# A two-layer decoder on one core: decay sums taken once in retention, context loads moved ahead, the first keys of head attention and its back projection moved

## What is computed

```
dt = softplus(x @ Wa + dt_bias); alpha = exp(-exp(A_log) * dt)
cum_log = cumsum(log(alpha + 1e-08), axis=1)            # over the 56 tokens, per head
log_l = cum_log[..., :, None] - cum_log[..., None, :]
l_mat = where(causal, exp(log_l), 0)
out = (einsum(q, k) * l_mat) @ v
```

## Time and profile before

| | |
|---|---|
| median of 3 runs | 1634.42 us (1632.02 to 1636.08) |
| profiled execution | 1648.23 us, its span 1646.4 us |
| PE busy in the span | 94% |
| retention, first block | 18 to 43 us |
| retention, slots | 43 to 101 us |
| gate and norm | 101 to 113 us |
| context attention | 113 to 291 us |
| head attention | 668 to 1431 us |

### The profile page before, as it was taken

How to read it: one execution, slowest core, us unless ns; L and a number is a source line. 1 busy time by engine, 2 the same in 40 slices (tenths; PEclk the granted TensorE clock), 3 DMA queues, 4 the chain that set the end, 5 groups by cost and what they waited for, 6 DMA issues and landing times. The chain is left out here.

```text
span 1646.4 us, 45308 instructions
## 1 busy us (share of the span) xinstructions
PE 1544.4 (94%) x16414; PEld 1193.2 (72%) x16414; DVE 1121.6 (68%) x1761; ACT 896.3 (54%) x1419; POOL 701.8 (43%) x755
## 2 busy tenths in 40 slices
PE   8998999989999987889999999999999999889998
PEld 4544666679989655457777777777777777668887
DVE  3643545668787468467777777777777777267777
ACT  5463333432222347346666666666666666467776
POOL 0300000577877456443444433444433444166665
PEclk9998999999999999799999999999999999999999
DMA  2028984131110000376655566655556654212211
GB/s 76 1 58 223 249 243 129 39 118 51 64 41 22 1 2 2 90 166 151 145 127 131 129 142 149 147 125 131 129 140 149 149 125 112 52 39 79 69 63 45
DMA packets 53548, 168.84 MB, mean 103 GB/s; under 512 B 12640, under 2 KB 25280, under 8 KB 53472
## 3 DMA queue, kind: packets, MB, share of 16 engines
q1 hardware_dynamic: 51312, 156.30, 38.0%
q10 hardware_dynamic: 2160, 11.52, 2.3%
HBM read 90.27 MB, written 1.03 MB: 55 GB/s over the span
## 5 line engine op out<-in xcount | busy, mean ns | idle before, releaser
L1907 DVE TENSOR_REDUCE hat_tops<-banks 128x1 f32<-128x500 f32 x672 | 442.0, 677 | 151.4 <-PE banks L1653 151.3
L1780 ACT ACTIVATE hat_pb<-banks 125x896 f32<-125x896 f32 x384 | 340.2, 916 | 226.3 <-PE banks L1672 222.2
L1653 PE MATMUL banks<-hat_kh,hat_qm 128*128 128x500 f32 x672 | 298.7, 462 | 3.8 <-DVE hat_tops L1907 3.5
L1672 PEld LDWEIGHTS banks<-hat_q,hat_k 128*125 128x125 f32 x1536 | 219.6, 188 | 74.4 <-issue 31.9
L1672 PE MATMUL banks<-hat_q,hat_k 128*125 128x224 f32 x1536 | 250.5, 286 | 15.8 <-ACT hat_pb L1780 9.2
L1849 POOL CAST hat_kh<-hat_kf 128x500 fp32r<-128x500 f32 x96 | 58.5, 609 | 404.1 <-ACT hat_kf L1793 389.3
L1663 PE MATMUL banks<-hat_pb,hat_vs 125*27 125x168 f32 (+1 forms) x6144 | 166.9, 261 | 0.1
L1663 PEld LDWEIGHTS banks<-hat_pb,hat_vs 125*27 125x27 f32 (+1 forms) x6144 | 132.1, 98 | 44.1 <-issue 24.4
L1226 ACT ACTIVATE ffn_rg<-banks 128x448 f32<-128x448 f32 x128 | 69.9, 546 | 165.6 <-PE banks L1159 165.5
L1653 PEld LDWEIGHTS banks<-hat_kh,hat_qm 128*128 128x128 f32 x672 | 127.7, 191 | 40.9 <-DVE hat_tops L1907 25.5
L2149 DVE TENSOR_TENSOR moe_hl<-moe_hf,moe_hh 128x448 fp32r<-128x448 f32 x128 | 108.5, 887 | 42.3 <-POOL moe_hh L2041 41.6
(11 more groups left out here) (286 smaller groups left out, 3091.3 us busy)
## 6 DMA issues: line engine op xcount, KB each, us to landing
hat_k<-hat_kh SPq DMA_DIRECT2D x256, 187.5 KB, 4.7
hat_ct<-ctxT SPq DMA_DIRECT2D x32, 750.0 KB, 6.2
hat_k<-hat_kl SPq DMA_DIRECT2D x128, 187.5 KB, 4.5
ctx_cx<-ctx SPq DMA_DIRECT2D x32, 672.0 KB
ctx_cd<-ctxT ACTq DMA_DIRECT2D x15, 750.0 KB, 5.7
ffn_cb<-expert_weights SPq DMA_DIRECT2D x8, 896.0 KB, 4.3
moe_cb<-expert_weights SPq DMA_DIRECT2D x8, 896.0 KB, 6.1
moe_raw<-Mw SPq DMA_DIRECT2D x18, 256.0 KB, 3.0
```

The source lines that it names most:

```text
L1653: peak_out.inc(nc.tensor.matmul(g.bank(PK + m % 2)[:, 0:SB], qm[u][:].rearrange("p h i -> p (h i)")[:, r * 128:r * 128 + 128], kh[u][:, c ...
L1672: mm = nc.tensor.matmul(g.bank(2 * (t % 2) + j // 2)[0:SW, (j % 2) * QW:(j % 2 + 1) * QW], k3[u][:, j, t * SW:(t + 1) * SW], q3[u][:, j, : ...
L1780: exped.inc(nc.scalar.activation(pb[t % 6][:].rearrange("p (n i) -> p n i", n=2), g.ps[0:SW, 2 * (t % 2):2 * (t % 2) + 2, 0:2 * QW], ACT.E ...
L1907: peaked.inc(v.tensor_reduce(tops[:, r, n:n + 1], g.bank(PK + m % 2)[:, 0:SB], AX_X, ALU.max))
```

## The change

It has five parts. (1) The running sums of `decay` are made for all pairs at once: one product by `until`, two copies of the sum (a rounded part and the remainder, `parts`), four transposes, a copy `turned`, a store of it to a DRAM tensor, and from there two small loads for each pair into rows 56 to 59 of `hid[u]`, which also holds the mask. The exponent of a pair is then `unit @ hid` plus `turned @ head_of`, four fp32r products; `after`, `upto`, `dm` and DVE's product are gone. (2) The slots of retention are written out in full. (3) The context loads of pairs 0 to 3 are issued by SP in retention's first block, ahead of the store. (4) In head attention the three key products of sequence 0 follow the first three query products, into banks 4 to 6, and ACT's key copies stand between its query copies; `keep_warm` at the end of causal attention goes. (5) Head attention's output matrix is applied to chunks 0 to 2 before the barrier, in place of the two `keep_warm`s, and the next norm does only chunk 3.

```diff
@@ Normal.on_pe
-            back(0)
-            back(1)
+            for c in range(self.early, max(self.early, 2)):
+                back(c)
         for c in range(CH):
-            if self.project:
-                pe.wait_ge(self.added, c + 1)
+            if self.project and c >= self.early:
+                pe.wait_ge(self.added, c + 1 - self.early)
@@ retention, first block, SP
+                ahead.first_loads(sp)
+                sp.wait_ge(sums_kept, 1)
+                sp.dma_start(g.sums_dram.rearrange("g r c -> r g c"), turned[:].bitcast(F32)).then_inc(sums_stored, 16)
+                sp.wait_ge(sums_stored, 16)
+                sp.wait_ge(cleared, 6)
+                for p in range(2):
+                    load_rows(sp, p)
@@ retention, first block, PE
                     if p == 8:
+                        pe.wait_ge(scaled, 3)
+                        pe.wait_ge(s_step, 6)
+                        nc.tensor.matmul(g.bank(4)[:, 0:PAIRS * H], c_["until"], decay[:]..., start=True, stop=True).then_inc(sums_out, 1)
...
+                pe.wait_ge(sums_split, 2)
+                for n in range(4):
+                    mm = nc.tensor.transpose(g.bank(5)[:, n * 128:n * 128 + 128], parts[:, 4 * n:4 * n + 4]..., c_["ident"])
+                mm.then_inc(sums_turned, 1)
@@ retention, second block, SP
+                for p in range(2, PAIRS):
+                    d_out.wait(sp, p - 2)
+                    load_rows(sp, p)
@@ load_rows
+            for k in range(2):
+                source = g.sums_dram[p // 4, 32 * (p % 4):32 * (p % 4) + 32, 64 * k:64 * k + L]
+                sp.dma_start(hid[p % 2][L + 2 * k:L + 2 * k + 2].bitcast(F32), source.rearrange("(l h) i -> l h i", l=2)).then_inc(rows_in[p % 2], 16)
@@ retention, second block, PE
                         exped.wait(pe, p - 1)
+                        pe.wait_ge(rows_in[u], 32 * (h + 1))
                         for k in range(2):
-                            nc.tensor.matmul(g.ps[:, 4 + k, 0:CW], unit[:], hidden[:], start=True, stop=False)
-                        dmade.wait(pe, p)
+                            nc.tensor.matmul(g.ps[:, 4 + k, 0:CW], unit[:], hid[u][:, 8 * k:8 * k + 8, :], start=True, stop=False)
                         for k in range(2):
-                            mm = nc.tensor.matmul(g.ps[:, 4 + k, 0:CW], c_["after"], dm[u][:, 8 * k:8 * k + 8, :], start=False, stop=True)
+                            mm = nc.tensor.matmul(g.ps[:, 4 + k, 0:CW], turned[own_rows, p // 4, :], head_of[own_rows, 8 * k:8 * k + 8, :], start=False, stop=True)
                         d_out.inc(mm)
@@ context_attention, first block
-            block.sync(first_loads)
@@ causal_attention, end of PE
-                keep_warm(g, 0, 2)
@@ head_attention, PE, query(c)
+                    if c == 0:
+                        pe.wait_ge(loaded[0], 16)
+                    if c < 3:
+                        pe.wait_ge(norm.logged, c + 1)
+                        k_out.inc(nc.tensor.matmul(g.bank(4 + c)[:, 0:SB], g.w["HWkT"][:], ct[0][:, c * SB:(c + 1) * SB], start=True, stop=True))
@@ head_attention, end of PE
-                exped.wait(pe, B - 1)
-                keep_warm(g, 0, 2)
+                normed.wait(pe, B - 9)
+                ends.on_pe(0, 4)
                 sum_weights(B - 1)
-                keep_warm(g, 0, 3)
+                ends.on_pe(1, 5)
+                ends.on_pe(2, 0)
@@ head_attention, end of DVE
                 pick(B - 1)
+                ends.on_dve(dve, 0, 4)
                 divide(B - 1)
+                ends.on_dve(dve, 1, 5)
+                ends.on_dve(dve, 2, 0)
                 normed.wait(dve, B - 1)
+                dve.wait_ge(ends.added, 3)
@@ head_attention, DVE at the start
-                norm.on_dve(dve)
+                norm.on_dve(dve, add_bias)
@@ experts_silu
-        norm = Normal(g, ctx, "n6", ..., g.obias[:, 0:1], split=True)
+        norm = Normal(g, ctx, "n6", ..., g.obias[:, 0:1], split=True, early=3)
```

More of the change, by code:

```diff
@@ L262, in on_dve @@
                 self.parts(dve, 0)
+            if then and c >= 1:
+                then(c - 1)
+        if then:
+            then(CH - 1)
     def parts(self, dve, c):
@@ L356, in _, with retention @@
             dve.wait_ge(normed, CH)
-def retention(g):
+def retention(g, ahead):
     nc, c_ = g.nc, g.c
@@ L582, in _ @@
             def _(dve):
-                give(dve, dmade, weighed)
+                give(dve, weighed)
                 def slot(p, u, h, scores, sums, outputs):
[L586 to L589, removed]
                     if sums:
@@ L661, in context_attention @@
         zt = g.xn
-        cx = [[sb(f"cx{w}{k}", [SW, ST, D]) for k in range(2)] for w in range(4)]
-        cd = [sb(f"cd{u}", [128, 3, SB]) for u in range(2)]
+        cx, cd, loaded, straight = ahead.cx, ahead.cd, ahead.loaded, ahead.straight
         ct = sb("ct", [128, 3, SB])
@@ L727, in slot @@
                         pved.wait(sp, p - 4)
-                        load(sp, p, w)
+                        ahead.load(sp, p, w)
                 four_ends(sp, slot)
@@ L1647, in peak @@
                         qm_made.wait(pe, q)
+                        if isinstance(q, int) and q == 0:
+                            k_full.wait(pe, q)
                     if r == 0:
@@ L1764, in _, with copy_keys @@
                 give(act, v_copied, k_full, exped, logged, inverted)
+                def copy_keys(p, n):
+                    k_out.wait(act, p, n + 1)
+                    k_low.wait(act, p - 1, n + 1)
+                    first = isinstance(p, int) and p == 0
+                    k_full.inc(nc.scalar.activation(kf[:, n * SB:(n + 1) * SB], g.bank(4 + n if first else MISC)[:, 0:SB], ACT.Identity, bias=g.w["Hbk"][:, 0:1]))
                 norm.on_act(act)
                 for c in range(CH):
+                    if c < 3:
+                        copy_keys(0, c)
                     act.wait_ge(q_full, c + 1)
@@ L1788, in copy_values @@
                                                 g.bank(MISC)[0:SW, :].rearrange("p (t h e) -> p t h e", t=4, e=DH)))
[L1790 to L1793, removed]
                 def slot(p, u, h, keys, maxima, sums):
+                    later_keys = keys and reached(p, 1)
                     for i in range(IT):
@@ L1803, in slot @@
                             copy_values(p - 1, 1 - u, 2)
-                        if i == 2 and keys:
+                        if i == 2 and later_keys:
                             copy_keys(p, 1)
@@ L1929, in _, with each_pair @@
                 pick(B - 1)
+                ends.on_dve(dve, 0, 4)
                 divide(B - 1)
+                ends.on_dve(dve, 1, 5)
+                ends.on_dve(dve, 2, 0)
                 normed.wait(dve, B - 1)
+                dve.wait_ge(ends.added, 3)
+def each_pair(engine, slot):
+    for p in range(PAIRS + 2):
+        slot(p, p % 2, p // 2, p < PAIRS, 1 <= p <= PAIRS, p >= 2)
 def staged(engine, n, slot):
```

135 lines of the change are left out of this document (97 added, 38 removed).

## The result

The changed kernel took 1675.97 us (median of 4 runs, 1666.34 to 1678.12) against 1634.62 us before: ratio 1.0229, 95% interval 1.0196 to 1.0263. That is 2.3% slower, where 1632 (1618 to 1641) was forecast.

What follows compares the result with a forecast made beforehand. PE, busy in 94% of the span, was taken as the bound. Retention +5.8, context attention -2.8, part 4 -2.6 and -0.1, part 5 -2.7 summed to -2.4 us: median 1632, range 1618 to 1641.

Steps and rivals of the forecast that it cites:

- the term for the clock: Retention's first slots: low clock after PE's 20 us of standing, costing 2 us (1 to 4).
- The clock staying low through the slots: Retention: listed as a sign that would make the forecast wrong; no size or chance given.
- Pace of 2.35: Retention's slots: 3.43 us a pair falls by 1.08 to 2.35, saving 17.3 us (14 to 19).
- The row loads never paced the slots: Retention rival, chance 0.1: row loads set the pace, 3.15 us a pair, loop gains 4.5, time 1645.
- Start of the slots: Retention: the store waits behind the context loads, so slots begin at 64.4, 21.1 us later (18 to 24).
- The store does not overtake the loads: Retention rival, chance 0.12: the store overtakes the context loads, slots start +6.9 instead of +21.1, time 1617.
- Context attention: Its slots: wait of 1.50 on `cd` goes, pair 9's `cx` wait stays; gain 2.8 us, between 1.5 and 4.2.
- Part 4: End of causal attention: without unused products the barrier opens 2.6 us earlier (0 to 2.6).
- The keys save nothing: Start of head attention: first scores still wait for the full DMA queue; gain 0.1 us.
- Part 5: End of head attention: barrier 1.3 us later, next norm 9.6 instead of 13.58; net -2.7 (-1 to -3.5).
- retention to the projection: Retention in all: start +21.1, pace -17.3, low clock +2.0, sum +5.8 us.

Runs made afterwards that it cites:

- late_warm: Changed kernel with context loads issued where the kernel before issues them, plus 8 unused 128-row fp32 products behind the transposes of the sums; ratio 1.0082.
- early_full_rows: Changed kernel, early context loads kept, with only the products of the sums with the head mask made 128 rows instead of 32; ratio 1.0055.
- full_rows: As late_warm, but the products of the sums with the head mask contract over 128 rows (zero-padded copies) instead of 32; ratio 0.9975.
- slot_warm: As late_warm, with one unused 128-row fp32 product ahead of each slot's masks; ratio 1.0022.
- the new profiles of before: Second and third profiles of the unchanged kernel before; spans 1633.3 and 1636.4 us, against 1646.4 in its first.
- parts45: Kernel before with only parts 4 and 5 of the change; retention and context attention as before; ratio 0.9995.
- old_retention: Changed kernel with retention's exponents made as before, in a loop, without sums, store or row loads; context loads stay early; ratio 1.0014.
- full_late_loads: full_rows with 12 unused products before the barrier, one in each of the first and last two slots, context loads behind the last row loads; ratio 1.0040.
- fp32_sums: Changed kernel with the products of the stored sums with the head mask read as fp32 (four passes) instead of fp32r; ratio 1.0416.

## Why the prediction was wrong

**The step that failed** is the term for the clock, "I expect the low clock for the first slots: 2 us (1 to 4)". "The clock staying low through the slots" stood among the signs of being wrong, but no rival had it with a price. The slots were to last 58.0-17.3+2.0=42.7 us; they lasted 67.0. These 24.3 us of 1.2 GHz, and 1.3 more at the gate (13.44 us to the projection, 12.12 before), are the miss. I treated the clock as a matter of entry: low after a wait, back soon. Shown instead: whether it comes back depends on what the slot is made of. Before, a slot had two more products of four passes on 128 rows; the change left the two mask products on 128 rows and everything else on 32 or 56. Such slots never got the upper level back once they had lost it, be it behind 21 us of standing or behind the short waits of the first slot (`late_warm`). With 128 rows in the same product it came back (`early_full_rows`, and `full_rows`, where it fell too, near 55), and with an unused 128-row product it was never lost (`slot_warm`). The entry has a price too, and it was put too low: with full rows and the cold entry the slots took 45.4 us (`early_full_rows`), not 42.7. Whether the changed slots would keep the level if no wait at all disturbed them was not tried.

The Trainium skill (TensorE: Matmul & The Clock Gate, Part 1: The HAM clock gate) says that the gate is set by how busy PE has recently been. By that rule these slots would run at full clock; the trace does not agree, 55.46 us busy of 56 at 0.50. The Trainium skill (TensorE: Matmul & The Clock Gate, Architectural detail: the array is 16× 32×32) says that the array is 16 sub-arrays of 32x32. If so, a product of 32 rows uses one of the four rows of them. That would fit the runs, and no run shows that it is the reason.

**Pace of 2.35: right**, at the clock that it was worked out for (`full_rows`). The row loads never paced the slots, also at 2.33.

**Start of the slots: right in mechanism.** 64.4 forecast, 62.52 and 66.05 measured: 21.4 and 25 us behind the new profiles of before, where 21.1 (18 to 24) was forecast. The store does not overtake the loads; it landed after 16.3 us in one profile and 19.9 in the other.

**Context attention: right in size, hidden in this pair.** -2.8 forecast, +2.4 read. Without any wait on `cx`, kernels with early loads took 159.1, 159.3 and 158.8 us for these slots, kernels with loads at before's place 161.8, 162.0, 161.6, 162.3 and 162.0: -2.8 between the means. The waits on `cx` come and go between executions, with early and with late loads: nine of the 17 profiles have 1.2 to 7.9 us of them (7.9 and 5.0 in the two of after, 6.9 in `full_rows`, 4.2 in `parts45`), eight have none. I had not counted that in the range. What they hang on was not tried.

**Context loads beside working slots have a price**, which the forecast didn't need, as the slots were to begin once the loads had drained: 2.58 us of stand and the low clock behind it, 5.5 us together (`old_retention` against `parts45`), more than the 2.8 that the early loads save. The expectation of `old_retention` had put it at nothing. The two ratios, 1.0014 and 0.9995, leave a loss of 3 us, as 5.5 less 2.8 does. In `full_late_loads` the stand is 4.78 us, and it is gone with the loads moved away; each of these is one profile. What PE waits for is not shown. That it is instructions, held up behind the loads, is a guess. The profile's DMA view has one transfer of a queue that it calls instruction just ahead of the first stand (53.3 to 53.4) and one in the middle of the second (96.2 to 96.4). It doesn't name the engine, and `parts45` has such a transfer between 51 and 52 without a stand.

**Part 4: right.** From the last weighing product to the next stage 3.39 us instead of 5.88 (-2.5; forecast -2.6). The keys save nothing: 27.4 us from the first spread DMA (717.00) to the first scores, 27.25 before.

**Part 5: half, and the clock has the other half.** From the last `sum_weights` to the first expert product 16.82 instead of 18.08: -1.3, forecast -2.7. The stage starts 30.1 later on the trace's scale while the last `sum_weights` is 28.3 later, +1.8 for the forecast 1.3. The norm took 10.5 instead of 9.6. Centring comes first and the one projection behind it at 1465.76, where I had it at the head, but that is not what costs: the two centring products run at the lower level (granted clock 0.51 from 1462.7 to 1465.7) behind a wait of 2.84 us, and take 3.19. In `old_retention` they kept the upper level behind the same wait:

```profile
1425.94 1.74 PE L243 MATMUL banks<-xt,constants 128*128 128x448 f32 x4 [2.84 <-PEq L2347]
```

There the norm took 9.1 us and the whole way 15.4, the forecast's -2.7. Over the profiles of all kernels with part 5, the two products take 1.74 to 3.3 us behind a wait of 2.8 to 2.9. Why one execution keeps the level there and another loses it was not tried.

Summed over the first pair of profiles: retention to the projection +29.5 (forecast +5.8), context +2.4, to HWq -3.7, scores +0.1, part 5 -1.3, the rest +0.4: +27.4. Against the new profiles of before, retention to the projection is +31.8 and +35.4: the start 21.4 and 25, the slots 9.1, the gate 1.3.

## What to carry to other kernels

Before fewer or smaller products are counted as a gain at full clock, look at how much of the remaining PE work uses all 128 rows. If a loop is left with 32- and 56-row products mainly, price it at half the clock as a rival of its own (here 4.09 against 2.35 us a pair), and try zero-padded full-row operands, which cost no pass. A transfer moved beside tight PE work isn't always free even where that work needs no data of it (5.5 us here), and a small store behind large loads on one queue waits for them (16.3 us against 2.3).

## What the runs showed of the hardware

A PE almost without a gap can stay at 1.2 GHz for 67 us (over 100 in `fp32_sums`, at 6.33 us a pair). With full-row products in the slots it came back from 21 us of standing within 7 us. One and the same wait of 2.84 us in front of the same two products can cost the level (3.19 us for the two, changed kernel) or not (1.74, `old_retention`). One profiled execution can stand 14 us above its kernel's median, spread over three stages; a comparison of two single profiles has that error.
